# Rows of weight scales carried to all partitions by DMA through DRAM, with a reordered front

## The reference

```python
def conv(x, c, weight, c_weight, bias):                 # x (128, 32, 512)
    out = conv1d(x, weight, groups=4, taps=9, padding=4)  # 32 channels, 8 to a group
    return out + (c @ c_weight.T)[:, :, None] + bias[None, :, None]

def fake_quant(t, axis):
    s = max(max(|t|, axis) / 127, 1e-8)
    return clip(round(t / s), -128, 127) * s

def qlinear(x, w):
    return fake_quant(x, axis=-1) @ fake_quant(w, axis=1).T

y = conv(x, cond_128, L0_cond_weight, L0_cond_c_weight, fside_S_0)
h = silu(qlinear(y, w_gate)) * qlinear(y, w_up)         # w_gate, w_up (1376, 512)
out = x + qlinear(h, w_down)                            # w_down (512, 1376)
```

## Time and profile before

| | us |
|---|---|
| median of 3 runs | 296.19 (296.0 to 296.42) |
| the profiled execution | 296.72 |
| its span | 295.1 |

### The profile page before, as it was taken

How to read it: one execution, slowest core, us unless ns; L and a number is a source line. 1 busy time by engine, 2 the same in 40 slices (tenths; PEclk the granted TensorE clock), 3 DMA queues, 4 the chain that set the end, 5 groups by cost and what they waited for, 6 DMA issues and landing times.

```text
span 295.1 us, 4775 instructions
## 1 busy us (share of the span) xinstructions
PE 280.5 (95%) x1607; PEld 164.7 (56%) x1633; DVE 251.6 (85%) x408; ACT 194.0 (66%) x231; POOL 199.9 (68%) x208
## 2 busy tenths in 40 slices
PE   7994999999999999999999999999999999999994
PEld 6883667654555555555444566656444444444443
DVE  3869769999999997988989878898988889889885
ACT  2276799998677667555787745444788866667640
POOL 1567849998777677553788846543777887667623
PEclk9999999999999999999999999999999999999999
DMA  7999922579968677955389997526366673333335
GB/s 263 416 412 360 413 62 61 116 164 227 250 173 182 169 164 136 231 161 132 110 204 310 222 269 205 134 79 92 103 155 158 156 195 94 87 86 84 103 98 196
DMA packets 83847, 53.36 MB, mean 181 GB/s; under 512 B 69904, under 2 KB 70672, under 8 KB 83696
## 3 DMA queue, kind: packets, MB, share of 16 engines
q1 hardware_dynamic: 83536, 52.89, 66.0%
q10 hardware_dynamic: 288, 0.18, 0.3%
HBM read 27.75 MB, written 8.39 MB: 122 GB/s over the span
## 4 chain that ended last, share of the span: by engine, by line
PE 75%; POOL 7%; DVE 5%; issue 5%; ACT 3%; DMA 3%; SPq 1%; POOLq 1%; DVEq 0%
PE bank L1021 43%; PE bank L1041 20%; PE bank L909 11%; DMA slab<-x_windows 3%; POOL sg_mem L504 2%; POOL hq_mem L456 2%; DVE h_mem L789 1%; DVE h_max L795 1%; POOL y_mem L483 1%; PE bank L925 1%; POOL xo_mem L512 1%; ACT y_mem L558 1%; ACT wgu_t L570 1%; SPq L315 1%; ACT gu_scale_row L580 1%
## 5 line engine op out<-in xcount | busy, mean ns | idle before, releaser
L1021 PE MATMUL bank<-wgu_t,xq_mem 128*128 128x512 bf16 (+1 forms) x745 | 154.0, 356 | 2.7 <-DVE h_mem L789 1.0
L504 POOL TENSOR_TENSOR sg_mem<-sg_mem,gu_scale_row 128x512 f32<-128x512 f32 (+1 forms) x96 | 111.3, 1162 | 65.4 <-ACT sg_mem L614 65.4
L1021 PEld LDWEIGHTS bank<-wgu_t,xq_mem 128*128 128x128 bf16 x768 | 74.1, 98 | 73.1 <-DVE h_mem L789 6.9
L614 ACT ACTIVATE sg_mem<-sg_mem,x_scale 128x512 f32<-128x512 f32 (+1 forms) x96 | 63.7, 674 | 44.1 <-DVE sg_mem L779 44.0
L1041 PE MATMUL bank<-wd_t,hq_mem 128*128 128x512 bf16 (+1 forms) x338 | 78.2, 379 | 0.2
L789 DVE SCALAR_TENSOR_TENSOR h_mem<-bank,x_scale,sg_mem 128x512 f32<-128x512 f32 (+1 forms) x96 | 66.3, 692 | 10.7 <-POOL sg_mem L504 9.8
L779 DVE TENSOR_TENSOR sg_mem<-bank,gu_scale_row 128x512 f32<-128x512 f32 (+1 forms) x96 | 60.3, 628 | 16.2 <-PE bank L1021 16.1
L619 ACT ACTIVATE h_mem<-h_mem,h_inv 128x1376 f32<-128x1376 f32 (+1 forms) x32 | 45.3, 1415 | 29.0 <-DVE h_inv L671 28.9
L1041 PEld LDWEIGHTS bank<-wd_t,hq_mem 128*128 128x128 bf16 (+1 forms) x341 | 33.4, 98 | 40.1 <-DMA hq_mem<-hq_mem 0.2
L795 DVE TENSOR_REDUCE h_max<-h_mem 128x1 f32<-128x1376 f32 x32 | 50.4, 1576 | 0.0
L909 PEld LDWEIGHTS bank<-toeplitz_cut,slab 128*128 128x128 f32 x320 | 43.2, 191 | 4.3 <-DMA slab<-x_windows 1.4
(11 more groups left out here) (62 smaller groups left out, 136.2 us busy)
## 6 DMA issues: line engine op xcount, KB each, us to landing
slab<-x_windows SPq DMA_DIRECT2D x32, 320.0 KB, 4.8
xo_mem<-x SPq DMA_DIRECT2D x24, 256.0 KB, 3.0
out<-xo_mem SPq DMA_DIRECT2D x24, 256.0 KB, 2.2
hq_mem<-w_gate_up SPq DMA_DIRECT2D x6, 512.0 KB, 6.7
slab<-w_down SPq DMA_DIRECT2D x3, 688.0 KB, 11.3
h_mem<-w_gate_up SPq DMA_DIRECT2D x4, 512.0 KB, 13.9
slab<-x SPq DMA_DIRECT2D x1, 2048.0 KB, 9.4
out<-slab SPq DMA_DIRECT2D x7, 256.0 KB, 2.0
```

Of the source, the lines that this page charges most:

```text
L504: pool.tensor_tensor(s, s, gu_scale_row[:, 1, at:at + n], ALU.mult).then_inc(silu_scaled, 1)
L614: act.activation(s, s, ACT.Silu, scale=x_scale[:, i:i + 1]).then_inc(silu_done, 1)
L1021: last = pe.matmul(bank[n % 2][:, 0:cols], xq_t[:, g, k, P * c:P * (c + 1)], wgu_t[:, m, k, at:at + cols], start=(k == 0), stop=(k == KT - 1))
```

## The change

Four things change.

- The third piece's part of `gu_scale_row` (weight tiles 8 to 10) no longer goes over PE and ACT. SP stores the scale columns of the three tiles to a DRAM tensor `gu_row_dram`, one word of 4 bytes per row of the weights (704 in all), waits for these stores, and loads the row from there to all partitions. DVE and POOL wait for this load (`gu_row_in`) where they waited for ACT's copy.
- `wd_scale_row` is made in the same way: the store stands in SP's turn of channel 3 (L457 after), the load in that of channel 4, behind the four residual loads (L440 after).
- The front is put in another order: rows of scales for the first piece earlier, spans 8 and 9 loaded ahead of weight tiles 8 to 10, span 9 and span 10 convolved earlier, the folds of group 0 ahead of weight tiles 6 and 7, tile 10's maximum and inverse between the first scalings of channel 0, POOL making four of the scales, and no 12 empty matmuls.
- Banks and waits follow from these.

The core of the diff:

```diff
@@ SP
+            load_span(SPANS)
+            load_span(SPANS + 1)
             load_w(8)
             load_w(9)
-            load_span(SPANS)
             load_w(10)
-            for q in range(SPANS + 1, SPANS + 4):
+            for q in range(SPANS + 2, SPANS + 4):
                 load_span(q)
...
             load_w_down(KT - 1)
+            sp.wait_ge(gu_scale_ready, JT - 1)
+            for j in range(LAST_FROM, JT - 1):
+                at = P * (j - LAST_FROM)
+                sp.dma_start(gu_row_dram[:, at:at + P].rearrange("m p -> p m"), gu_scale[:, j, :],
+                             allow_slow_non_contiguous=True).then_inc(gu_row_out, 16)
+            sp.wait_ge(gu_scale_ready, JT)
+            sp.dma_start(gu_row_dram[:, LAST_COLS - TAIL:].rearrange("m p -> p m"), gu_scale[0:TAIL, JT - 1, :],
+                         allow_slow_non_contiguous=True).then_inc(gu_row_out, 16)
+            sp.wait_ge(gu_row_out, 16 * (JT - LAST_FROM))
+            sp.dma_start(gu_scale_row[:, :, LAST_FROM * P:],
+                         bass.AP(gu_row_dram.tensor, 0, [[0, P], [LAST_COLS, 2], [1, LAST_COLS]])).then_inc(gu_row_in, 16)
...
                     for t in range(XO_BUFS):
                         load_residual(t)
+                if i == DOWN_ROW_AT + 1:
+                    sp.wait_ge(wd_row_out, 16)
+                    sp.dma_start(wd_scale_row[:, :], bass.AP(wd_row_dram.tensor, 0, [[0, P], [1, L]])).then_inc(wd_row_in, 16)
...
+                if i == DOWN_ROW_AT:
+                    sp.wait_ge(d_scale_ready, KT)
+                    sp.dma_start(wd_row_dram[0, :].rearrange("(t p) -> p t", p=P), d_scale[:, :],
+                                 allow_slow_non_contiguous=True).then_inc(wd_row_out, 16)
@@ POOL
+            def scale_w(j, n):
+                assert j in SCALED_BY_POOL
+                r = rows(j)
+                pool.wait_ge(gu_max_ready, j + n)
+                pool.tensor_scalar(gu_scale[0:r, j:j + n, :], gu_max[0:r, j:j + n, :], 1.0 / QMAX, SMALLEST_SCALE,
+                                   ALU.mult, ALU.max).then_inc(gu_scale_ready, n)
...
-                if i == 0:
+                if i == 0 and p < 2:
                     pool.wait_ge(xq_copied, use("scales", p, 1) + 1)
+                elif i == 0:
+                    pool.wait_ge(gu_row_in, 16)
@@ ACT
-            def copy_down_row():
-                act.wait_ge(wd_row_turned, 1)
-                act.activation(wd_scale_row[:, :], down_bank[1][:, :], ACT.Copy).then_inc(wd_row_copied, 1)
...
-            copy_xq(5)
-            copy_xq(6)
@@ DVE
             weights_top(4)
+            fold_y(3)
             weights_top(5)
-            weights_scale(4, 2)
-            fold_y(3)
+            fold_y(5)
             weights_inverse(4, 2)
-            weights_top(6)
             add_shift(6)
-            weights_top(7)
             add_shift(7)
-            weights_scale(6, 2)
-            fold_y(5)
-            weights_inverse(6, 2)
             fold_y(7)
             group_top(0)
             group_scale(0)
             group_inverse(0)
+            weights_top(6)
+            weights_inverse(6, 1)
+            weights_top(7)
...
+                elif i == 0:
+                    dve.wait_ge(gu_row_in, 16)
...
             def scale_down(i):
                 if i == 0:
-                    dve.wait_ge(wd_row_copied, 1)
+                    dve.wait_ge(wd_row_in, 16)
...
+                else:
+                    weights_top(JT - 1)
                 scale_gate(i, 1)
+                if i == 0:
+                    weights_inverse(JT - 1, 1)
@@ PE
-            run_empty(12)
...
                 if i == 0:
                     turn_gate_up(8)
                     gate_or_up(i, 1, 1)
                     turn_gate_up(9)
+                    conv_span(10)
                     turn_gate_up(10)
-                    conv_span(9)
-                    turn_xq(5)
-                    turn_xq(6)
...
-                if i == DOWN_ROW_AT:
-                    turn_down_row()
```

## The result

The changed kernel takes **320.87 us** (median of 4 runs, 319.37 to 321.3) against 296.10 for the kernel before on the same chip (295.89 to 296.42): ratio 1.0827, 95% interval [1.0806, 1.0848]. The forecast was 305.5 with a range of 300.2 to 308.9. The direction was right, the size was not: +24.8 us, where +9.3 was forecast. The profiled execution has a span of 319.4 us, against 295.1.

The account below looks back on a forecast made before the run. It took PE to bound the kernel, with little slack on DVE. Waits for the third piece's row (+4.5, front's gain included) and w_down's row (+4.8) sum to 9.3 on 296.19, giving 305.5 us, range 300.2 to 308.9.

Parts of the forecast that it names:

- the one on the stores: Front, third piece's row: the three stores land 1.3 us behind the queue's backlog, at 41.5; bounds nothing to 3 us.
- words of 4 bytes are written far slower than any row here: Rival on the third piece's stores: first row comes after 48, total above 309 us; chance 0.06.
- a store in channel 3, hidden, since SP waits there for ACT: w_down's row: its added store was claimed to be hidden in SP's existing wait for ACT.
- The backlog to 40.2: Front, SP's queue: loads ahead of the stores end with w_down's last tile, issued at 25.91, landing at 40.2.
- The first row in at 44.8 with a wait of 5: Channel 0: load issued at 41.5 takes 3.3, row in at 44.8; DVE idle some 5 us, end +4.5.
- The chain of 6.6 us to the end of `multiply_up(1, 0)`: Channels 0 to 1: cross-engine chain from the start of `scale_gate(0, 2)` takes 6.6 us, where before it took 7.25.
- The wait of 6.4 for w_down's row: Channel 4, `scale_down(0)`: row lands at 77.2, DVE wants it at 70.84, so waits 6.4 us; end +4.8.
- The slack of 1.57: Channel 5: PE needs `multiply_up(5, 0)` at 77.41, it ended at 75.84; this 1.57 us comes off DVE's second wait.
- The new front at -0.6 us: Front: the reordering gains 0.6 us where the row is there in time; `scale_gate(0, 2)` starts at 39.7.

Follow-up runs that it names:

- e5: Changed kernel with the stored words 64 bytes apart and the row loads reading w_down instead, so scales are wrong; 307.0 us (ratio 1.0377).
- e6: e2 with the loads of the last two w_down tiles and spans 12 to 15 moved behind the row's load; 304.41 us (1.0286).
- e1: Changed kernel's new front alone, both rows of scales by TensorE and ScalarE as in the kernel before; 295.12 us (0.9968).
- e12: The same version as e1, measured a second time in more rounds; 294.99 us (0.9969).
- e4: Kernel before plus five probe stores of w_down's scales that nobody waits for, in different layouts and channels; 296.6 us (one run).
- e11: Kernel before plus two unawaited probe stores of words side by side: 512 on ACT's queue, 256 on SP's; 296.52 us (single run).
- e7: e1 with w_down's row through DRAM in 16-byte runs, stored and loaded early, DVE reading it at a stride of 4 words; 300.29 us (1.0149).
- e2: Changed kernel with w_down's row by TensorE and ScalarE again, the third piece's row still through DRAM; 306.27 us (1.0328).

## Why the prediction was wrong

**The step that failed** is the one on the stores: "bounded from below they cost nothing behind the 40.2, from above 3 us ... without its issue time that is 1.3, and I take this: 41.5". I bounded 704 words of 4 bytes by a store of 128 KB, that is, by bytes, because no row had such a write. They landed at 46.33, 4.8 us later. The upper end of 3 us was too low as well, and the rival "words of 4 bytes are written far slower than any row here", given 0.06, is the one that came true. What makes them slow is not their size: the same words 64 bytes apart (e5) landed at 40.3, below my 41.5. Nor is it the backlog alone: without it the words side by side still took 7.4 us of their own (e6).

**The same step, in channel 3**: "a store in channel 3, hidden, since SP waits there for ACT". The store's issue is hidden; its landing is not. My load was to be issued at 71.65 + 4.5 = 76.1 and to land at 81.7; it landed at 96.2. The 14.5 are: 5.8 by which SP came there later, since the first hole was longer than forecast (10.4 for 4.5), 4.4 of SP's wait for the store, a wait that I had written off, and 4.3 since the load took 9.9 and not 5.6 us, with taps, windows and residuals held ahead of it.

**What held, and what held by luck.** The other steps can be read in e5, where the neighbourhood of the words is gone:
- The backlog to 40.2: the load was issued at 40.29.
- The first row in at 44.8 with a wait of 5: 44.54 and 5.1. Here two errors cancel: the stores landed 1.2 us earlier than my 41.5, and the load took 4.2 us and not 3.3.
- The chain of 6.6 us to the end of `multiply_up(1, 0)`: 6.17 in e5 and 6.16 in the changed kernel, so 0.4 too long in the forecast.
- The wait of 6.4 for w_down's row: 6.5. Both waits together put DVE's scaling at 81.58, forecast 70.84 + 4.5 + 6.4 = 81.74. Again two errors cancel: SP issued the load at 74.73 and not at 76.1, and it took 6.8 us and not 5.6.
- The slack of 1.57: `multiply_up(5, 0)` ends 10.75 us later in e5, 1.57 off is 9.2; the span grew by 9.7.
- The new front at -0.6 us: -1.1 (e1 and e12). `scale_gate(0, 2)` starts at 39.40 in e1 (39.7 forecast), the first gate product at 28.63 in the changed kernel (29 to 30 forecast).

The Trainium skill, DMA: Bandwidth & Descriptors, "Anatomy of one DMA", puts most of a DMA's fixed cost into the receipt of the write in the target memory. The windows with 0 GB/s from 42 to 46 us agree with a write that is issued and not confirmed; the page's 2 us, fitted on GpSimd's path, do not hold for these words, which SP issues. Its "Specifications" say that below 512 B a transfer does a read-modify-write. Taken alone, by size, that would make words 64 bytes apart as slow as neighbours; e4 shows 3.7 us for the former, so the rule misses what decides here. That words within one piece of memory are written one after the other is an explanation and not shown: no run shows the memory itself. It fits the words in all runs, but by itself it doesn't say why runs of 16 bytes, which share such pieces too, land in 1.6 to 2.5 us.

## What to carry to other kernels

A small store is priced by how its *writes* lie in DRAM, not by its bytes: ask of every small store whether it writes single words of many partitions side by side, and if so, space them by 64 bytes or store each partition's words as one run. Such a store is not only its own cost: what was issued within a few microseconds of it, on SP's queue or on ACT's, landed late with it. And a small store behind a full queue waits for the queue, however its words lie (e5). A cost that no row of the trace shows needs an upper end from a mechanism, not from the nearest size; a chance of 0.06 was too little for the one term without a row.

## What the runs showed of the hardware

- 512 words side by side in DRAM: 9.4 to 10.9 us to landing, 256 words 7.9, the 704 words of the third piece, in three stores, 11.1 to 13.7 each behind the full queue, 6.0 to 8.3 each without the backlog (e6). Issue to landing less the 1.6 us of the store in runs is 15 ns a word for the 512 of e11 and 25 for its 256. In e6 the second and third store land 2.8 and 2.1 us behind the one before, 11 ns a word.
- The same 2 KB 64 bytes apart 3.7 us (2.2 in e5), 512 bytes apart 2.9, in 16-byte runs 1.6 to 2.5, into SBUF 2.3 for each 512 bytes.
- Transfers on another engine's queue (a transpose on SP's, 6.6 us for 3.1), and loads issued half a microsecond earlier (5.8 for 2.8 in e11, 7.2 for 2.9 in e4), are held as well.
- A DVE `scalar_tensor_tensor` in f32 with one operand read at a stride of 4 words: 1159 ns for 744. The Trainium skill, VectorE: DVE Perf Modes, "Mode 1× (REGULAR) — the baseline", says that in this mode weird strides work and one result comes a cycle; in e7 the stride cost 56% more.
- In the changed kernel PE was idle from 40 us on; the granted clock was at 0.57 in 42 to 44 and at 0.50, the 1.2 GHz level, from 44 to 54. Such a fall cost some 0.3 us in e2.
